# Router front of a macaron block: logits from a transposed x, variance by Square, ranks chunk by chunk

## The reference

```
gate_scores = softmax(x @ Wg)                    # x is the layernormed row, Wg [256, 8]
topk_scores, topk_idx = top_k(gate_scores, 2)    # made to sum to 1
fused = silu(x @ W11[e]) * (x @ W12[e])          # 512 wide
out = sum over the two e of score * (fused @ W2[e])
```

## Time and profile before

| | us |
|---|---|
| median of 3 runs | 1039.33 (1038.33 to 1042.59) |
| profiled execution | 1031.17 |
| its span | 1029.4 |
| PE busy | 919.6 (89%) |
| DVE busy | 600.6 (58%) |
| ACT busy | 330.0 (32%) |
| POOL busy | 602.4 (59%) |

### The profile page before, as it was taken

One profiled execution on the slowest core, in us unless ns is written; L12 is line 12 of the kernel. 1 busy time (PEld: TensorE's weight loads), 2 busy tenths in 40 slices (PEclk: granted clock), 3 DMA queues, 4 the chain that ended last, 5 costly groups with the idle time before them and its releaser, 6 DMA issues.

```text
span 1029.4 us, 20399 instructions
## 1 busy us (share of the span) xinstructions
PE 919.6 (89%) x5412; PEld 794.1 (77%) x5413; DVE 600.6 (58%) x1478; ACT 330.0 (32%) x655; POOL 602.4 (59%) x549
## 2 busy tenths in 40 slices
PE   7957999999999999984997995399999999999995
PEld 6945878888888888873775684388888888888884
DVE  5486656656556465536766885855555555555552
ACT  3431333424334332221226541023233223322321
POOL 4104766767667677743214770157777777777773
PEclk9999999999999999997999996599999999999998
DMA  9435466464573754323212547234344343343332
GB/s 345 141 103 185 77 173 159 81 191 108 139 190 57 195 131 92 57 27 108 62 41 61 185 143 317 89 87 73 58 78 68 57 78 55 72 76 58 52 49 30
DMA packets 75970, 111.86 MB, mean 109 GB/s; under 512 B 11792, under 2 KB 60816, under 8 KB 75600
## 3 DMA queue, kind: packets, MB, share of 16 engines
q0 software_dynamic: 31808, 37.83, 23.8%
q1 hardware_dynamic: 31744, 49.82, 14.3%
q10 hardware_dynamic: 12368, 23.61, 6.6%
HBM read 66.79 MB, written 48.63 MB: 112 GB/s over the span
## 4 chain that ended last, share of the span: by engine, by line
PE 66%; DVE 12%; DMA 6%; issue 5%; POOL 4%; ACTq 3%; ACT 3%; POOLq 0%; DVEq 0%; SPq 0%
PE bank L1254 34%; PE bank L1277 16%; PE bank L1263 5%; PE bank L1246 3%; DMA x_rows<-yb,idx_i 3%; PE bank L1182 2%; PE bank L1371 2%; DVE work L787 2%; DMA xn_rows<-work 1%; DVE bnst L775 1%; POOL seq L438 1%; DVE sg L947 1%; DVE work L861 1%; ACT sg L617 1%; DVE w_lo L1019 1%
## 5 line engine op out<-in xcount | busy, mean ns | idle before, releaser
L947 DVE TENSOR_TENSOR sg<-sg,bank 128x512 f32<-128x512 f32 x142 | 97.7, 688 | 303.3 <-ACT sg L617 303.3
L1254 PE MATMUL bank<-w_hi,xt_hi 128*128 x568 | 241.8, 426 | 17.8 <-DVE xt_lo L936 15.9
L1254 PE MATMUL bank<-w_hi,xt_lo 128*128 x568 | 225.3, 397 | 0.0
L1254 PE MATMUL bank<-w_lo,xt_hi 128*128 x568 | 223.6, 394 | 0.0
L449 POOL DMA_INDIRECT xg<-xn_rows,idx_i x142 | 144.3, 1016 | 116.4 <-DVE idx_i L875 73.8
L609 ACT ACTIVATE yb<-bank,gates_in 128x256 f32<-128x256 f32 x142 | 67.3, 474 | 448.6 <-DMA out_rows<-yb,idx_i 216.6
L453 POOL DMA_INDIRECT gates_in<-gate_rows,idx_g x142 | 136.4, 961 | 52.0 <-issue 41.7
L1277 PE MATMUL bank<-w_hi,ft_hi 128*128 x568 | 159.4, 281 | 7.2 <-ACT yb L609 7.2
L462 POOL DMA_INDIRECT x_rows<-yb,idx_i x71 | 115.4, 1626 | 77.1 <-DMA x_rows<-yb,idx_i 36.1
L1277 PE MATMUL bank<-w_hi,ft_lo 128*128 x568 | 160.1, 282 | 0.0
L1277 PE MATMUL bank<-w_lo,ft_hi 128*128 x568 | 159.9, 282 | 0.0
(11 more groups left out here) (209 smaller groups left out, 1249.5 us busy)
## 6 DMA issues: line engine op xcount, KB each, us to landing
xn_rows<-work SPq DMA_DIRECT2D x16, 512.0 KB, 2.8
w_lo_rows<-w_lo ACTq DMA_DIRECT2D x16, 512.0 KB
w_lo<-w_lo_rows SPq DMA_DIRECT2D x16, 512.0 KB
work<-x_rows SPq DMA_DIRECT2D x16, 512.0 KB, 3.7
w_lo<-w_lo_rows SPq DMA_DIRECT2D x2, 4096.0 KB, 17.8
x_all<-x SPq DMA_DIRECT2D x8, 512.0 KB, 8.2
w_lo_rows<-in_sb ACTq DMA_DIRECT2D x16, 256.0 KB, 2.4
out_rows<-seq SPq DMA_DIRECT2D x8, 512.0 KB, 3.3
```

Of the source, the lines that this page charges most:

```text
L947: nc.vector.tensor_tensor(sg[p], sg[p], ps_g[p][:], ALU.mult).then_inc(f_step, 1)
L1254: last = nc.tensor.matmul(dst[p][:], xt[p][:, c, :], of(w), start=(c == 0 and n == 0), stop=(c == DC - 1 and n == len(parts) - 1))
```

## The change

`x` is given a second time as `xt`, transposed [256, 4096]; it is loaded into the free parts of `seq` and `gate`, one half issued by SP, in turn with the chunks of x, the other by ACT. PE makes the logits from it directly, with a ninth column of 1/256 in Wg that gives the mean. The transposes, ACT's copies of them and DVE's bn_stats of round 0 go. DVE copies logits and mean out of PSUM; ACT computes the variance by Square with the mean as bias and an accumulated sum. Ranks are counted within each pair of chunks and started from a running sum of the chunks before, so that the place within the tile is made for three of the four groups before the last chunk is in. The tile part stays in the router, with the product by partition on ACT. SP's load of expert 0 goes ahead of the stores of chunks 6 and 7, the copy of x behind all of them. `fold()` goes behind the ranks, its copies out of PSUM into the first expert tile. The second router keeps its instructions.

```
             for k in range(NCH):                                     # SP
+                sp.dma_start(xt_raw[0][:, chunk k], xt[0:P, chunk k]).then_inc(xt_in[k], 16)
                 load_x(k)
...
-            sp.dma_start(x1_dram[0:L, :] ..., x ...).then_inc(x1_out, 16)
             for k in range(NCH):
+                if k == NCH - 2:
+                    sp.wait_ge(order_ready, 1)
+                    e = expert_of_slot(sp, 0)
+                    load_up(sp, 0, e)
+                    load_down(sp, e)
                 sp.wait_ge(norm_ready, k + 1)
                 sp.dma_start(rows(xn_dram, k), xn[k % 2]).then_inc(xn_out[k % 2], 16)
+            sp.dma_start(x1_dram[0:L, :] ..., x ...).then_inc(x1_out, 16)
...
+            for k in range(NCH):                                     # ACT, first of all
+                act.dma_start(xt_raw[1][:, chunk k], xt[P:D, chunk k]).then_inc(xt_in[k], 16)
...
+            def variance_x(k):
+                act.wait_ge(x_all_in[k], 16)
+                act.wait_ge(neg_ready, k + 1)
+                if k > 0:
+                    act.wait_ge(var_ready, k)
+                for t in range(k * G, (k + 1) * G):
+                    last = nc.scalar.activation(bank[t % G // 2][:, t % 2 * D:(t % 2 + 1) * D], x_all[:, t, :], ACT.Square,
+                                                scale=D ** -0.5, bias=x_neg[:, t:t + 1], accum_out=x_var[:, t:t + 1])
+                last.then_inc(var_ready, 1)
             for k in range(NCH):
-                rows_t(k, k % 2)
+                variance_x(k)
                 if k > 0:
-                    logits_out(k - 1, k - 1)
                     apply_x(k - 1, (k - 1) % 2)
             apply_x(NCH - 1, (NCH - 1) % 2)
+            tiles_by_p()
             router_exp(0)
...
+            def tiles_by_p():
+                for g in range(NQB):
+                    act.wait_ge(oh_ready, g + 1)
+                    if g >= 2:
+                        act.wait_ge(inv_used, g - 1)
+                    nc.scalar.activation(pair_tile_x[g % 2][:, 0], at_tile[g % 2], ACT.Copy, scale=p_plus_1[:]).then_inc(by_p_ready, 1)
+                    if g > 0:
+                        (high_up, high_value, high_down)[g - 1](0)
...
+            def places_x(g):                                         # DVE
+                dve.wait_ge(ranks_x, 2 * g + 2)
+                nc.vector.tensor_tensor(picked_rank, onehot[:, :, here, :], ps_k[g % 2] ..., ALU.mult).then_inc(placed, 1)
+                ... reduce_sum to rank; rank_up, whole, place_x from it
+                nc.vector.tensor_tensor(at_place[g], place_row ..., place_x ..., ALU.is_equal)
...
+            def router_x():
+                dve.wait_ge(counted, 1)
+                ... sizes, order (order_ready), first, in_slot, pairs, first_16, picked_first, first_of_q, tile_x of groups 0 to 2
+                for g in range(NQB):
+                    if g == NQB - 1:
+                        places_x(g)
+                        link(... tile_x of group 3 ...)
+                    if g >= 2:
+                        dve.wait_ge(inv_used, g - 1)
+                    nc.vector.tensor_tensor(at_tile[g % 2], place_row ..., across(tile_x), ALU.is_equal).then_inc(oh_ready, 1)
+                    dve.wait_ge(oh_ready, g + 1)
+                    nc.vector.tensor_tensor(pair_tile_x[g % 2][:, 1], at_tile[g % 2], across(tile_of_q[:]), ALU.mult).then_inc(first_step, 1)
+                ends_of(sorted_)
+                ... the logits less their maximum, times rstd
+                indices(0)
...
             for k in range(NCH):                                     # DVE
-                stats_x(k, k % 2) ... top2(0, ...)
+                top2_x(k)                                            # two copies out of PSUM, then as top2
+                if k % 2 == 1:
+                    sum_chosen(k // 2)
+                if k in (3, 5, 7):
+                    places_x((k - 3) // 2)
+            router_x()
...
             for k in range(NCH):                                     # PE
-                transposes_x(k); route_chunk(k - 1, ...); ranks(...)
+                logits_x(k)                                          # 8 matmuls of 9 columns
+                if k > 0:
+                    ranks_of(k - 1)
+            count()
+            ranks_of(NCH - 1)
+            fold()
             router(0)
```

More of the change, by code:

```diff
@@ L510, in _ @@
             act.dma_start(col[:], cols).then_inc(s_cols, 16)
+            for k in range(NCH):
+                act.dma_start(xt_raw[1][:, k * CH:(k + 1) * CH], xt[P:D, k * CH:(k + 1) * CH]).then_inc(xt_in[k], 16)
             act.wait_ge(s_cols, 16)
@@ L807, in top2, with counts @@
                 nc.vector.tensor_tensor(chosen[:, here, :], onehot[:, 0, here, :], onehot[:, 1, here, :], ALU.add).then_inc(chosen_ready, 1)
-            def router(r):
+            def counts(cnt):
+                shift, tiles, sorted_, first = (small[:, at_:at_ + E] for at_ in (0, 8, 17, 25))
+                link(nc.vector.tensor_scalar(shift, cnt, P / 2 - 0.5, up_to_tile, ALU.add, ALU.add))
+                link(nc.vector.tensor_scalar(tiles, shift, -up_to_tile, float(P), ALU.add, ALU.max))
+                return tiles, sorted_, first
@@ new lines, in ends_of @@
+            def ends_of(sorted_):
+                ends, past = (small[:, at_:at_ + E] for at_ in (41, 49))
+                link(nc.vector.tensor_tensor_scan(ends, ssm[:, ONE:ONE + 1].to_broadcast([P, E]), sorted_, 0.0, ALU.mult, ALU.add))
+                link(nc.vector.tensor_scalar(past, ends, -1.0 / P, None, ALU.mult))
+                nc.vector.tensor_scalar(tile_ends[:], ends, 1.0 / P, None, ALU.mult)
+                link(nc.vector.tensor_tensor(past_end, place_row[:, 0:ET, 0:1].to_broadcast([P, ET, E - 1]),
+                                             past[:, 0:E - 1].unsqueeze(1).to_broadcast([P, ET, E - 1]), ALU.is_le))
@@ L821, in router @@
-                shift, tiles, sorted_, first, first_e, ends, past = (small[:, at_:at_ + E] for at_ in (0, 8, 17, 25, 33, 41, 49))
+                nc.vector.tensor_tensor(lg, lg, vals[:, :, 0:1].to_broadcast([P, NT, E]), ALU.subtract).then_inc(below_max, 1)
+                first_e = small[:, 33:33 + E]
                 pairs = small[:, 64:128].rearrange("p (j e) -> p j e", e=E)
                 one = ssm[:, ONE:ONE + 1].to_broadcast([P, E])
-                up_to_tile = float(3 * 2 ** 29)
                 link(nc.vector.memset(small[:, 16:17], 0.0))
-                dve.wait_ge(ranks_done, r + 1)
@@ L827, in router @@
[L827 to L838 removed]
+                dve.wait_ge(ranks_done, 1)
@@ L1225, in ranks, with ranks_of, count @@
                                           start=False, stop=(t == NT - 1))
-                if t1 == NT:
-                    mm.then_inc(ranks_done, 1)
+                mm.then_inc(ranks_done, 1)
+            def ranks_of(k):
+                chosen, n, g = route_mem[0][3], QB // TOPK, k // 2
+                if k % 2 == 0:
+                    if g >= 2:
+                        pe.wait_ge(placed, g - 1)
+                    if g >= 1:
+                        pe.wait_ge(sums_ready, g)
+                    else:
+                        pe.wait_ge(chosen_ready, k + 1)
+                        pe.wait_ge(wg_ready, 1)
+                    nc.tensor.matmul(ps_k[g % 2], ones, chosen_sum[:, g:g + 1, :].to_broadcast([P, n, E]), start=True, stop=False)
+                pe.wait_ge(chosen_ready, k + 1)
+                for t in range(k * G, (k + 1) * G):
+                    i = t % n
+                    mm = nc.tensor.matmul(ps_k[g % 2][:, i, :], before, chosen[:, t, :], start=False, stop=(i == n - 1))
+                    if t == 0:
+                        mm.then_inc(ye_done, 1)
+                    if i < n - 1:
+                        nc.tensor.matmul(ps_k[g % 2][:, i + 1:n, :], ones, chosen[:, t:t + 1, :].to_broadcast([P, n - 1 - i, E]), start=False, stop=False)
+                mm.then_inc(ranks_x, 1)
+            def count():
+                pe.wait_ge(sums_ready, NQB)
+                nc.tensor.matmul(ps_n[:, 0:E], ones, chosen_sum[:, NQB, :], start=True, stop=True).then_inc(counted, 1)
             def router(r):
```

284 lines of the change are left out of this document (165 added, 119 removed).

## The result

The changed kernel took 1035.33 us (median of 7 runs, 1030.73 to 1038.16) beside 1042.23 us for the kernel before (7 runs on the same chip, 1038.33 to 1044.99): a ratio of 0.9937, 95% interval 0.9909 to 0.9964, faster by 6.6 us. It was timed twice more with the experiments: 1030.99 us, 0.9908 (0.9882 to 0.9935), and 1031.62 us, 0.9906 (0.9885 to 0.9928). So the change is worth some 6.6 to 9.8 us; 12.6 were forecast and the time given was 1027.0.

What follows compares the result with a forecast made beforehand. PE's chunks, then DVE's router, were taken to bound the front, with ScalarE late after the change. 12.6 us off the profiled 1031.17 gave 1018.6; 8.2 more for the runs' median gave 1026.7, stated as 1027, range 1018 to 1034.

Steps and rivals of the forecast that it cites:

- four signs of being wrong: First one-hot on DVE after 50, loads under 300 GB/s, gathers of over 5 us, another pace in the tiles.
- inv_done from 77.77 to 65.15: End of the router stage: comes 12.6 us earlier, the whole gain forecast.
- The copy lands between 62 and 67, and the first gather is at 66.5: Copy of x behind the last store: 8 to 13 us alone; at worst 17.5, gathers sharing with it for 5.
- Rival (b): ScalarE heavier or copy collides: Squares at 1.0, 6 more, 1033; gathers beside the copy up to 5 more, 1032; chance 0.18.
- From there the same pace: Expert tiles: from the first expert matmul, near 71.6 us, the pace stays as before.
- ScalarE's last apply at 52 to 55: ScalarE's chunk work: no gap from 31.2, when chunk 0's store lands, then 22.4 us, ending at 53.6.
- four Squares: Variance on ScalarE: 0.62 us each taken, 2.5 us a chunk; 2.0 to 3.0 for four would show it right.
- First one-hot: DVE in the router: first one-hot of tiles at about 45 us, before at 63.8.
- PE's last logits at 35.2: PE's chunk stretch: eight chunks of 3.28 us and six rank counts of 0.45 from 6.3, ending at 35.2.
- Rival (a): ScalarE lighter or stall shorter: Squares at 0.4, 1023; store of chunk 0 landing by 25 in addition, 1018; chance 0.2.
- Rival (c): Loads at the start run at a lower rate; at 150 GB/s chunk 0's store lands 21.6 later, 1048; chance 0.05.
- Rival (d): Removed work isn't the path; something unseen holds the first tile near 80 us, time 1035 to 1040; chance 0.07.

Runs made afterwards that it cites:

- e3: Changed kernel with the gate weights' tile `wg_sb` allocated behind all other tiles; 1033.09 us, ratio 0.9906 to the kernel before.
- e5: Changed kernel with the product by partition (tiles_by_p) moved from ACT back to DVE; 1031.49 us, ratio 0.9893 to the kernel before.
- e7: Changed kernel with the copy of x in eight pieces of 1 KB rows, each behind its chunk's store; 1022.68 us, ratio 0.9903 to the kernel before.
- e1: Kernel before with the gate weights' tile 8 bytes wider per partition and xt as an unused input; 1041.41 us, ratio 1.001.
- e4: Changed kernel with the stores of normalised chunks issued by ACT instead of SP; 1032.98 us, ratio 0.9912 to the kernel before.
- e14: Changed kernel with the copy of x still one DMA behind the last store, in 1 KB instead of 32 KB runs; 1031.67 us, ratio 0.9913.
- e9: Kernel before with only the copy of x cut into eight pieces, each behind its chunk's store; 1026.68 us, ratio 0.9934.
- e2: Changed kernel with the copy of x back between the loads and the pads; 1041.3 us, ratio 0.9998 to the kernel before.
- e6: Changed kernel with ACT issuing the stores and the copy of x early, behind the loads; 1035.54 us, ratio 0.9942 to the kernel before.
- e11: Changed kernel with the product on DVE and eight copy pieces, all behind the stores of chunks 2 to 5; 1027.1 us, ratio 0.9861 to the kernel before.
- e8: Changed kernel with eight copy pieces, each behind its chunk's store, and the product by partition on DVE; 1020.96 us, ratio 0.9896.
- e10: Kernel before with xt declared as an input and never read, tiles and copy as before; 1033.82 us, ratio 1.0007.

## Why the prediction was too optimistic

The direction and the length of the router's front came out, and what bounds the router; the gather behind it and the pace of the tiles did not. The time was 8.3 us above the 1027.0 and outside 1018 to 1034 in the first comparison. Of these 2.6 us are the starting point: the forecast stood on a median of 3 runs, 1039.33, and the seven give 1042.23. With the same 12.6 us taken from each session's runs of the kernel before, the forecast would be 1029.6, 1028.0 and 1028.4; measured were 1035.33, 1030.99 and 1031.62, so 5.7, 3.0 and 3.2 us are left. Two of the prediction's four signs of being wrong came: gathers of over 5 us, and another pace in the tiles. Step by step:

- **inv_done from 77.77 to 65.15: right.** 64.07, and in one session 77.09 to 64.94, 12.15 us for 12.6.
- **The copy lands between 62 and 67, and the first gather is at 66.5: the step that failed.** The gather was at 65.4 to 66.2, but the copy landed at 71.2, 17.6 us after its issue (18.6 and 18.2 in the other two), where I took 8 to 13 as if it had the engines alone. It took 16.8 to 20.2 us at every place in the program where it was one piece. Its packets show of what: in the changed kernel the first began 3.8 us after the issue, behind the weights of expert 0 and the last stores, and all 64 took 13.4 us (12.6 to 15.7 in twelve profiles). So even its moving alone is at the upper end of what I took, and the time before its first packet I had left out. The gather costs 5.76, 6.47 and 6.31 us in place of 3.04, 3.02: 2.7 to 3.5 us on the path, that I had put at 0 and, as the worst, at 5. The gather's end is the copy's end, to 0.2 us, in all five profiles that have the one-piece copy in long runs behind the last store (71.15 and 71.2; 72.7 and 72.5; 72.6 and 72.4; e3 71.8 and 71.65; e5 73.8 and 73.6). e7 takes it away (3.06) and the first sigmoid comes 3.4 us earlier, though its time doesn't show it; e5 makes it 9.91. Rival (b)'s second half held with a chance that was too small and a price (1032) close to what was seen.
- **From there the same pace: not quite.** Round 1 is 0.021 us a tile slower in the trace, some 1.5 us a round, and e1 shows the same with nothing but a wider tile. The prediction had no term for where buffers lie. The times don't resolve it. 12.15 - 3.45 is 8.7 us, close to the 9.6 and 9.4 us measured in two sessions; two rounds more off, 5.7, and it is what the two spans of the table differ by (5.6). The first comparison has 6.6. Which is the better value can't be told from these runs, and what makes the first comparison lower is open.
- **ScalarE's last apply at 52 to 55: right by two errors that cancel.** It ended at 53.1 for 53.6. The store of chunk 0 landed at 32.8 for 31.2: it was issued only at 24.94, behind SP's issues of loads, so the sum of bytes gave nearly the right end for a queue in which the wait was before the issue. Then 19.9 us for 22.4: four Squares took 1.97 us for 2.5. The Trainium skill (ScalarE: Activation LUTs, What ACT_TABLE_LOAD costs) gives 280 ns + 0.833 ns an element with a bias pointer, 493 for this one; the trace agrees within 7% for the Square itself, 0.46 to 0.48 busy and 0.49 from start to start, and shows an accumulator read of 0.19 that hides between two of them.
- **DVE: right.** First one-hot at 45.5 (45), by_p 1.14 to 1.24 (1.15), DVE idle 8.0 us before the third.
- **PE's last logits at 35.2: 37.2,** since the third chunk's half of xt came 1.9 us late. It didn't matter: ACT was later.
- **Rival (a),** a shorter stall: e4 made it true (0.89 us instead of 7.54) and gained 1.7 us in the front beside e3 of its session (75.2 for 76.9), since the last store met the copy instead. **Rival (c),** a lower load rate: no, 382 GB/s from 10 to 15 us and 361 from 15 to 25, beside the 349 of the earlier trace rows. **Rival (d),** that something else is the path: not as I had it, but e5 shows that right behind the router stands a second limit, the copy's landing. **Rival (b)** was two things; Squares of 1.0 us are refuted (0.49), and "gathers beside the copy up to 5 more, 1032" is what came, at 3.

The prediction placed the copy behind the last store and asked when it would be done; it had the gather wait for nothing. The Trainium skill (DMA: Bandwidth & Descriptors, Queues, rings and completion order) says that an engine takes turns between queues packet by packet, and I drew from it that a gather on POOL's queue would not wait for the end of the copy. The measurement decides against that use of the rule: with the gather on another queue it landed with the copy five times in five, and e4's store on ACT's queue 2.4 us after it. The rule itself isn't refuted by the changed kernel: 1.95 us after the gather's issue, when its packets could have begun, all but four of the copy's 64 were done or under way, at some 3 us each. e14 is harder on it: its packets take 0.05 us, and the gather's first one still came 1.5 us late (69.27 for 67.73). Whether what the page calls a packet is one record of the trace isn't known here. The same section says that a completion is written only after every earlier write of that engine, whatever the queue; in the changed kernel the gather's own packets were late, 68.66 for 67.34, so the order of completions is at most a part of it.

How the front's gain divides between the copy's move and the rest (the transposed x, the ranks chunk by chunk and ACT's part of the router) isn't shown: e9's 6.5 us are for the greater part the clock's. In the kernel before, the stall of 14.59 us in the chain held PE for 0.80 us only, since PE had other work until 34.9; the prediction names the store as the chain's first piece and doesn't say how little hung on it. What is shown is e2: the rest without the copy's move brings nothing, because the stall on the store of chunk 0 grows to 19.62 us.

## What to carry to other kernels

A large transfer that "nobody waits for" has a price at every place: a small transfer that is issued behind it, on whatever queue, should be counted as landing with it or shortly before, so place it by its end, or cut it into pieces that are through before the next small transfer that matters. When a stall goes, look for the limit that stands a few us behind it: here taking work off ACT (e5) or the wait off its stores (e4) brought little, because the copy held what came next. A row's duration beside a transfer is not its own: the 14.59 us of the store was the copy's time. A wait in the chain costs only what it keeps the bound engine idle, here 0.80 us of 14.59. And before a difference between two executions is put down to an edit, compare the lengths of equal matmuls in them: the clock made 6.1 of e9's 6.5 us.

## What the runs showed of the hardware

- A copy of 4 MB within DRAM took 16.8 to 20.2 us in every profile that has it in one piece, and what was issued behind it on SP's, ACT's or POOL's queue landed about when it did: stores of 0.5 MB after 14.70 (e4), 17.14 (e6) and 17.79 us (e2) where one takes 2.8 alone, gathers of 128 KB after 5.8 to 9.9 where one takes 3.0. In pieces of 0.5 MB, a store behind one piece took 3.1 to 3.5 us (e7) and behind two or three of them 6.7 to 7.0 (e11), with the gather free.
- Of a gather's 3.0 us alone, 1.95 pass before its first packet (e2).
- An issue on SP's queue took 6.14 us (6.40 in e8) with the loads of x and xt ahead, where one takes 0.43 to 0.6, and a store behind it was late before it was even issued. A full queue would explain it; no run here varied it.
- TensorE's clock in the front isn't the same from execution to execution. In e9 16 logit matmuls took 1.85 us at 36.74 and 3.42 in e10 at 37.40, at the granted clocks shown above; in the second profile of the kernel before the higher level came at 28.4 (16 in 2.05 us), and from 31.9 PE stood idle for 3.25 us.
- A shift of 8 bytes in where buffers lie changed the spacing of matmuls from 117.35 to 118.4 ns, 1%.
